# Moving dt, output and first-half jobs to other slots of a Mamba chunk's timetable

## The reference

```python
xz = jnp.einsum('bld,ed->ble', x, in_proj)
xi, z = jnp.split(xz, 2, axis=-1)                 # 512 channels each
xi = silu(conv(xi))                               # 4 taps, per channel
dt, Bm, Cm = jnp.split(xi @ x_proj, [64, 80])
dt = softplus(dt @ dt_w + dt_b)
dA  = exp(dt[..., None] * A)                      # 16 states per channel
dBx = (dt * xi)[..., None] * Bm[:, :, None, :]
def step(h, inp):                                 # along the sequence
    a, bx, c = inp
    h = a * h + bx
    return (h, einsum('bds,bs->bd', h, c))
y = (ys + xi * Dp) * silu(z)
return y @ out_proj.T                             # 256 outputs, then a sigmoid
```

## Time and profile before

| | us |
|---|---|
| median of 3 runs | 4899.49 |
| lowest and highest of them | 4898.61, 4899.88 |
| the profiled execution | 4895.79 |
| its span | 4894.0 |
| outside the span | 1.8 |

### The profile page before, as it was taken

One profiled execution on the slowest core, in us unless ns is written; L12 is line 12 of the kernel. 1 busy time (PEld: TensorE's weight loads), 2 busy tenths in 40 slices (PEclk: granted clock), 3 DMA queues, 4 the chain that ended last, 5 costly groups with the idle time before them and its releaser, 6 DMA issues. The chain is left out here.

```text
span 4894.0 us, 64824 instructions
## 1 busy us (share of the span) xinstructions
PE 4398.5 (90%) x23652; PEld 3225.3 (66%) x23652; DVE 3895.3 (80%) x4126; ACT 3364.0 (69%) x5797; POOL 3321.6 (68%) x1558
## 2 busy tenths in 40 slices
PE   7888888888888888888888888888789999999999
PEld 3666556555655656666665666665678888888888
DVE  6999999999999989999999999999954454545452
ACT  7888777788888777787877778888534444444443
POOL 5999999999999999999999999999930000000000
PEclk9999999999999999999999999999899999999999
DMA  7433333333333333333333333333430101101000
GB/s 262 153 125 126 122 117 120 114 123 124 124 125 118 131 113 121 118 116 124 120 122 116 117 114 119 119 122 110 141 124 31 35 31 33 33 30 35 27 30 9
DMA packets 190688, 500.71 MB, mean 102 GB/s; under 512 B 16608, under 2 KB 101344, under 8 KB 155744
## 3 DMA queue, kind: packets, MB, share of 16 engines
q1 hardware_dynamic: 189472, 485.01, 29.7%
q10 hardware_dynamic: 896, 11.54, 0.7%
HBM read 460.83 MB, written 47.19 MB: 104 GB/s over the span
## 5 line engine op out<-in xcount | busy, mean ns | idle before, releaser
L1375 DVE TENSOR_TENSOR_SCAN m_h<-bank,m_state,m_dBx 128x512 f32<-128x512 f32 x1512 | 1854.5, 1265 | 117.5 <-ACT bank L1105 107.3
L831 PEld LDWEIGHTS bank<-ident,m_h 128*128 128x128 f32 x8192 | 981.9, 144 | 743.2 <-issue 381.2
L831 PE MATMUL bank<-ident,m_h 128*128 128x128 f32 x8192 | 1251.0, 280 | 220.3 <-DVE m_h L1383 189.1
L1270 POOL TENSOR_TENSOR m_h<-m_h,m_Cs 128x1024 f32<-128x1024 f32 x384 | 909.1, 2371 | 227.6 <-ACT m_state L1037 226.9
L1259 POOL TENSOR_TENSOR m_dBx<-u,m_Bs 128x1024 f32<-128x1024 f32 x432 | 1013.6, 2373 | 2.2 <-issue 0.2
L1259 POOL TENSOR_TENSOR m_dBx<-m_u,m_Bs 128x1024 f32<-128x1024 f32 x432 | 1013.3, 2373 | 2.1
L1383 DVE TENSOR_TENSOR m_h<-m_h,bank 128x1024 f32<-128x1024 f32 x640 | 764.9, 1195 | 25.9 <-PE bank L813 25.1
L1105 ACT ACTIVATE bank<-m_dt,cols 128x512 f32<-128x512 f32 x864 | 591.4, 687 | 237.1 <-DVE m_h L1375 235.3
L1105 ACT ACTIVATE bank<-dt,cols 128x512 f32<-128x512 f32 x864 | 591.2, 687 | 230.2 <-DVE m_h L1375 228.4
L302 POOL TENSOR_TENSOR mvj<-mvj,norm_c 128x4 f32<-128x4 f32 x16 | 16.5, 1033 | 982.2 <-DVE mvj L263 982.2
L813 PEld LDWEIGHTS bank<-ident,m_Ct 128*128 128x128 f32 x2560 | 292.5, 139 | 534.7 <-DVE m_h L1383 358.3
(11 more groups left out here) (176 smaller groups left out, 5937.5 us busy)
## 6 DMA issues: line engine op xcount, KB each, us to landing
m_Bs<-b_dram SPq DMA_DIRECT2D x256, 1024.0 KB, 4.7
m_Cs<-c_dram SPq DMA_DIRECT2D x384, 256.0 KB, 3.5
xx<-in_x SPq DMA_DIRECT2D x16, 512.0 KB, 5.9
xn_dram<-xx SPq DMA_DIRECT2D x16, 512.0 KB, 4.5
yb_dram<-m_ysb SPq DMA_DIRECT2D x16, 512.0 KB, 4.4
xx<-xn_dram SPq DMA_DIRECT2D x16, 512.0 KB, 3.8
x_dram<-m_ysb SPq DMA_DIRECT2D x16, 512.0 KB, 4.4
base<-xn_dram SPq DMA_DIRECT2D x16, 512.0 KB, 3.9
```

The source lines that it names most:

```text
L831: mm = pe.matmul(YB[b][:, o:o + P], h[:, k % NH, m, tok:tok + P], ident[:, :], start=(s == 0 and o == 0), stop=False, is_transpose=True, s ...
L1270: pool.tensor_tensor(o, o, Cs[:, i % 2, :].unsqueeze(1).broadcast_to((P, 2, T)), ALU.mult).then_inc(S["weigh_p"], 1)
L1375: dve.tensor_tensor_scan(o, decays, share, initial, ALU.mult, ALU.add).then_inc(S["scan"], 1)
```

## The change

Only numbers in the tables change. The third and fourth dt products go to slots 42 and 46 (from 43 and 49), the first half's sums to 60 and 61 (from 46 and 47), so that their gates stand in DVE's slots 62 and 63 (from 48 and 49). The first half of the output product goes to slots 33 to 36 (from 32 to 35), the second to slots 44 to 47 (from 38 to 41), so that its Tanh stands in ACT's slot 50 (from 44). The turn of C goes to slot 38 (from 37). The second dt product gets the other PSUM bank. The z products of the very first chunk go to other slots of the prologue.

```diff
-AT = {J_LN: (0, 1), J_X: (3, 5, 7, 9), J_CONV: (11, 16, 20, 24), J_DT: (35, 40, 43, 49), J_Z: (50, 52, 56, 57),
-      J_Y: (46, 47, 13, 17), J_OUT: (32, 38), J_UT: (26, 29)}
+AT = {J_LN: (0, 1), J_X: (3, 5, 7, 9), J_CONV: (11, 16, 20, 24), J_DT: (35, 40, 42, 46), J_Z: (50, 52, 56, 57),
+      J_Y: (60, 61, 13, 17), J_OUT: (33, 44), J_UT: (26, 29)}
...
-AT_B, AT_C = 29, 37
+AT_B, AT_C = 29, 38
...
-BANK = (0, 1, 0, 1, 0, 1, 0, 1, 0, 1, 1, 1, 1, 1, 1, 0, 1, 0, 1, 1, 0, 1, 0, 0, 0, 1, 0, 0)
+BANK = (0, 1, 0, 1, 0, 1, 0, 1, 0, 1, 1, 1, 0, 1, 1, 0, 1, 0, 1, 1, 0, 1, 0, 0, 0, 1, 0, 0)
...
-FIRST_Z = (33, 46, 38, 52)
+FIRST_Z = (33, 48, 37, 52)
```

## The result

The changed kernel takes 5197.4 us (median of 4, 5191.5 to 5199.4), the kernel before 4899.1 us (median of 4). The ratio is 1.0607, with a 95% interval of 1.0589 to 1.0626. The kernel became slower, as forecast, but by 298 us instead of 199, and above the range that ended at 5165. The profiled execution's span is 5189.7 us.

The account below looks back on a forecast made before the run. DVE, busy 93% of the chunk window, was taken as the bound. Slot 55's delay 4.8, gates 1.2 and PE's clock 0.6 made 6.6 us per chunk, times 30, plus some 2 us: 5098 us, range 5048 to 5165.

Parts of the forecast that it names:

- Part 2: ACT, slots 45 to 55: the second Tanh adds 0.48 us per chunk, three uncovered table loads 4.2 us.
- rival (d): A table switch on ACT costs more than the load: 5224 us, or 5212 by the skill page; chance 0.03.
- Rival (e): Third load on ACT falls away if Ln's set also has Exp: 5.2 us per chunk, 5056 us; chance 0.03.
- Rival (c): PE's lower clock lasts through slots 60 to 63: 8.4 us per chunk, 5152 us; chance 0.2.
- part 1: Chain of PE and ACT to slot 44: slot 44 starts 0.9 us sooner, ACT's following stretch 0.1 us later.
- Part 4: PE's lower clock after idling ahead of slot 56, making DVE wait ahead of slot 60: 0.6 us more per chunk.
- part 3: Two gates moved to DVE's slots 62 and 63, without idle time there: 1.2 us per chunk, lower end 0.6.
- The prologue: Moved z products ahead of DVE's first scan: put at nothing, since that scan waits there for other work.

Follow-up runs that it names:

- e3: The kernel before with one 128x1 Tanh more in ACT's slot 50, which brings the same three table loads: 5058.8 us.
- e1: The changed kernel with three matmuls more on PE at the end of slot 41, results overwritten: 5113.0 us.
- e10: The changed kernel with the first output product back at slots 32 to 35: 5097.0 us.
- e4: The kernel before with only the first half's turned sums and gates moved, to slots 60 and 61 (62 and 63 on DVE): 4921.7 us.
- e2: The changed kernel with a plain copy in place of the second Tanh per chunk, so without the three extra loads: 5022.4 us.
- e5: The changed kernel with a copy for the second Tanh and three matmuls more on PE at the end of slot 41: 4958.8 us.
- e6: The changed kernel with output product, turn of C and banks as before; only dt products and first-half sums at new slots: 4948.9 us.
- e11: The changed kernel with the second output product at slots 41 to 44, its Tanh ahead of the load for Exp and Ln: 5021.2 us.
- e8: The kernel before without six of the eight matmuls of the second output product (slots 39 to 41): 4845.9 us.
- e9: The changed kernel with one matmul more on PE at the end of slot 41, result overwritten: 5154.8 us.

## Why the prediction was wrong

**Right.** *Part 2*, the largest term. ACT's stretch from its first uB copy to the decay of slot 55 was put at 16.98 + 0.48 + 4.2 = 21.7 us; it took 21.73 us (2747.00 to 2768.73), and the same in the mean of the steady chunks. The waits on ACT came to 10.1 us, and the longest is slot 55's, 3.39 us. The three extra loads are there in 30 chunks. The Trainium skill's 2.66 us for a switch ("ScalarE: Activation LUTs", "What ACT_TABLE_LOAD costs") and with it rival (d) did not come true: e3 has all three loads and costs 5.2 us per chunk, of which about 1 us is the wait ahead of slot 60, where three switches at the page's price would be 8.0 us. Rival (e), two loads instead of three, fell by the count: the second Ln and the decay behind it have a load each. Rival (c) named PE's lower clock as a way to 5152, but for slots 60 to 63, where DVE waits 1.29 us ahead of slot 60 and not at all behind it.

**Wrong: part 1, the chain to slot 45.** The forecast read off correctly that PE would be done some 2 us sooner and that ACT's copies would then be last. It did not ask what PE does in the meantime. The step "slot 44 starts about 0.9 us sooner ... ACT's stretch starts 0.1 us later" took PE's durations from the earlier trace rows, where PE had idled 0.60 us; now it idled 3.11 us, and they nearly doubled. Instead of 0.1 us, ACT's stretch started 2.55 us later in the mean (5.46 after the end of scan 43, before 2.91). Part 4 had the very mechanism, but looked for it only ahead of slot 56, where the trace of before showed it. e1 prices the step at 84 us: with full clock the stretch starts 0.33 us later than before (3.24), slot 44 waits 1.25 us as forecast, and the time of 5113 us is back inside the range. That it then comes within 15 us of 5098 is in part luck, since the gates cost less than was put and slot 38 more.

**Wrong: slot 38.** The last quarter of the first output product moved into slot 36, ahead of `fill_a` of unit 19. The forecast said nothing of this wait; it is 0.55 us per chunk. That the first Tanh and so the copies come later was counted. e10 gives 100 us for undoing this one slot, far more than the 17 us of the wait itself; the other 83 are the earlier copies and PE's clock together.

**Mis-sized: part 3, the gates.** 1.2 us per chunk were put, e4 gives 0.6, the lower end. The reason named for that end, a gate that falls into a wait, is not what e4 shows: DVE's waits at slots 46 to 55 grow by 1.0 us, and the rest comes back mostly ahead of slot 60, where PE has the lower clock less often. The prologue, put at nothing, cost 4 us (first scan at 75.5 instead of 71.5 us).

**Part 4, PE's clock ahead of slot 60.** Put at 0.6 us more; the mean wait went from 0.66 to 1.29 us in the changed kernel. The size is right, though the lower clock came in 24 of the 29 steady chunks and not in each. In e3, where it came in all, the wait is 1.7 us.

**The account in us:** loads with what hangs on them 175 (e2), the lower clock ahead of slots 44 and 45 84 (e1), less 21 by which these two overlap (e5); the dt products 30 (e6 less e4), the gates 20 (e4). Three terms are estimates from waits and starts, times 30 chunks: slot 38 adds 17 (0.55 each), the moved Tanh 14 (the stretch takes 17.46 us in e2 and 16.99 before), and the earlier copies, which e6 does not have, take off 26 (slot 44 waits 1.26 us in e1 and 2.14 before). The sum is 293, against 298 measured. The forecast had 141 for loads and Tanh, 36 for the gates, 18 for the clock and 3 for the chain.

## What to carry to other kernels

One Tanh put between the load for Exp and Ln and the functions that used it brought three loads here: its own, one at the next Ln and one at the next Exp behind that. Look in the compiled order for the loads, and price them on the engine's own queue if another engine waits for its next result. When work is moved off an engine ahead of a wait, ask how long this engine then idles, and read the durations behind the wait from a place with a like idle time: on PE they nearly doubled here. Spare matmuls in an idle stretch right ahead of a chain that ends last can be worth more than the time they take.

## What the runs showed of the hardware

Ahead of the chain to slots 44 and 45, PE's clock fell behind idle times of 2.24 us and more, in a part of the chunks or in all, and hardly ever behind shorter ones. Below, the longest idle time of PE ahead of this chain (median), and in how many of the 29 steady chunks a 128x128 matmul of `fill_a` of unit 22 then took over 0.4 us (0.27 at full clock, 0.42 at 1.2 GHz):

| run | PE idle ahead, us | chunks with the lower clock |
|---|---|---|
| e1 | 0.53 | 0 |
| before | 0.60 | 0 |
| e11 | 1.54 | 3 |
| e8 | 1.75 | 0 |
| e9 | 2.24 | 19 |
| e10 | 2.62 | 20 |
| after | 3.11 | 29 |

In e11 PE has a second, shorter wait and other work between the idle time and the chain, so its row compares less well. The length of the idle time alone does not decide. Ahead of slot 56 the mean granted clock of the 5 us behind it is under 0.97 in none of the 29 chunks of e2 (1.70 us of idle time, median), in 15 of the kernel before (2.10), in 11 of e11 (3.42) and in all 29 of e3 (4.94).

A table load took 1.283 us in every run and at each place, and one of them sets the next activation back by 1.41 us, or 1.42 us by the difference between the changed kernel and e2; nothing beyond that shows.
